# A four-layer graph network kernel: GpSimd's gathers wait for TensorE's signal of two or three batches before

## What is computed

```python
x = _layernorm(x + _L0_gnn_ref(x, edge_index, ...))                 # mean of x[src] over the edges of a node, then a matmul
x = _layernorm(x + _L1_gnn_ref(x, edge_weight, src, dst, ...))      # max over the edges of relu([x[src], x[dst], w] @ W1 + b1) @ W2 + b2
x = _layernorm(x + _L2_gnn_ref(x, edge_index, ...))                 # an edge gate, sigmoid of a small MLP, weighs a normalised sum
x = _layernorm(x + _L3_gnn_ref(x, edge_index, ...))                 # attention, 4 heads of 32, softmax over the edges of a node
```

## Time and profile before

| what | us |
|---|---|
| median of three runs | 5461.31 |
| the profiled execution, time | 5471.71 |
| its span, first to last instruction | 5470.0 |
| TensorE matmuls, busy | 3630.2 |
| VectorE, busy | 3535.5 |
| GpSimd, busy | 3508.5 |
| ScalarE, busy | 1505.4 |
| gathers of the sum pass, first to last start | 5.2 to 1046.7 |
| of the max pass | 1212.5 to 2261.3 |
| of the gate pass | 2469.9 to 3510.5 |
| of the attention pass | 4268.2 to 5309.4 |

### The profile page before, as it was taken

One profiled execution on the slowest core, in us unless ns is written; L12 is line 12 of the kernel. 1 busy time (PEld: TensorE's weight loads), 2 busy tenths in 40 slices (PEclk: granted clock), 3 DMA queues, 4 the chain that ended last, 5 costly groups with the idle time before them and its releaser, 6 DMA issues. The chain is left out here.

```text
span 5470.0 us, 86641 instructions
## 1 busy us (share of the span) xinstructions
PE 3630.2 (66%) x19277; PEld 2699.7 (49%) x19277; DVE 3535.5 (65%) x7296; ACT 1505.4 (28%) x3630; POOL 3508.5 (64%) x3697
## 2 busy tenths in 40 slices
PE   4444333466666666677888888766656688888883
PEld 3333333344443444345666666555542466666662
DVE  6555222227888878615777777799883466666667
ACT  1111111132222222232222222266664122222222
POOL 7777777667777777647777777500006777777763
PEclk7555555568888888765555555598885677777775
DMA  7555555436666667426666666599983676677761
GB/s 234 182 183 180 188 186 179 140 92 198 206 209 208 207 208 207 138 63 164 172 170 170 171 170 169 140 307 306 290 277 116 190 215 213 214 212 218 215 187 50
DMA packets 832058, 1031.70 MB, mean 189 GB/s; under 512 B 233279, under 2 KB 544079, under 8 KB 831954
## 3 DMA queue, kind: packets, MB, share of 16 engines
q1 hardware_dynamic: 482964, 483.11, 29.0%
q0 software_dynamic: 144320, 323.10, 22.6%
q10 hardware_dynamic: 204670, 224.39, 11.6%
HBM read 668.65 MB, written 361.50 MB: 188 GB/s over the span
## 5 line engine op out<-in xcount | busy, mean ns | idle before, releaser
L513 POOL DMA_INDIRECT L_gath<-tab,src x832 | 796.4, 957 | 256.5 <-issue 250.9
L513 POOL DMA_INDIRECT L_gath<-in_x,src x832 | 789.1, 948 | 255.9 <-issue 251.8
L513 POOL DMA_INDIRECT L_gath<-tab_kv,src x832 | 788.9, 948 | 253.6 <-issue 240.2
L513 POOL DMA_INDIRECT L2a_gath<-tab_h,src x832 | 788.3, 947 | 253.8 <-issue 253.8
L616 DVE TENSOR_TENSOR_SCAN L_acc<-L_mask,L_acc,L_pT 128x512 f32<-128x512 bf16 x414 | 527.5, 1274 | 568.5 <-PE L_pT L574 567.5
L1386 POOL DMA_INDIRECT N_got<-run,last x196 | 190.0, 969 | 664.2 <-POOLq L116 605.6
L633 ACT ACTIVATE L_back<-L_pB 128x512 f32<-128x512 f32 x624 | 364.3, 584 | 894.5 <-PE L_pB L604 888.5
L574 PE MATMUL L_pT<-ident,L_gath 128*128 128x128 f32 x832 | 227.4, 427 | 558.9 <-DMA L_gath<-in_x,src 550.0
L604 PE MATMUL L_pB<-ident,L_acc 128*128 128x128 f32 x2496 | 522.8, 349 | 0.8 <-DVE L_acc L616 0.5
L604 PEld LDWEIGHTS L_pB<-ident,L_acc 128*128 128x128 f32 x2496 | 412.1, 185 | 154.0 <-issue 151.9
L574 PEld LDWEIGHTS L_pT<-ident,L_gath 128*128 128x128 f32 x832 | 146.3, 214 | 637.8 <-DMA L_gath<-in_x,src 340.1
(11 more groups left out here) (283 smaller groups left out, 7276.5 us busy)
## 6 DMA issues: line engine op xcount, KB each, us to landing
run<-L_back ACTq DMA_DIRECT2D x416, 256.0 KB, 4.0
L_seed<-seed SPq DMA_DIRECT2D x416, 256.0 KB
run<-L_back ACTq DMA_DIRECT2D x208, 264.0 KB
L_mask<-same SPq DMA_DIRECT2D x416, 128.0 KB, 3.9
seed<-L_zeros SPq DMA_DIRECT2D x208, 256.0 KB, 4.0
sent<-L2a_gath ACTq DMA_DIRECT2D x208, 256.0 KB, 2.9
L_sent<-sent SPq DMA_DIRECT2D x208, 256.0 KB, 4.6
run<-L_back SPq DMA_DIRECT2D x208, 256.0 KB, 4.5
```

Source lines behind the costliest of these rows:

```text
L513: gp.indirect_dma_start(out=gath[k][:, t, :], out_offset=None, in_=table, in_offset=bass.IndirectOffsetOnAxis(ap=g["src"][:, tile:tile + 1 ...
```

## The change

`gatherer` takes a second semaphore and a distance. From batch 32 on (`PACED = 32`) it waits, behind the wait for a free buffer and ahead of the marker, until batch n - 2 is signalled by TensorE (n - 3 in the max pass). In the sum and gate passes the semaphore is the one that frees the buffers too, `s_turn`; in the max pass it is `s_turn` instead of `s_sent`, in the attention pass `s_query` instead of `s_pv`. Nothing else changes: the same instructions on the same engines in the same order, with the same buffers.

```diff
+PACED = 32
...
-def gatherer(gp, g, table, gath, s_gath, s_go, s_free, s_copied=None):
+def gatherer(gp, g, table, gath, s_gath, s_go, s_free, s_pace, ahead, s_copied=None):
...
         room(gp, s_free, n, depth)
+        if n >= PACED:
+            room(gp, s_pace, n, ahead)
         gp.sem_inc(s_go, 1)
...
-            gatherer(gp, g, d["x"], gath, s_gath, s_go, s_turn)
+            gatherer(gp, g, d["x"], gath, s_gath, s_go, s_turn, s_turn, 2)
...
-            gatherer(gp, g, g["tab"], gath, s_gath, s_go, s_sent)
+            gatherer(gp, g, g["tab"], gath, s_gath, s_go, s_sent, s_turn, 3)
...
-            gatherer(gp, g, g["tab_h"], gath, s_gath, s_go, s_turn, s_aside)
+            gatherer(gp, g, g["tab_h"], gath, s_gath, s_go, s_turn, s_turn, 2, s_aside)
...
-            gatherer(gp, g, g["tab_kv"], gath, s_gath, s_go, s_pv)
+            gatherer(gp, g, g["tab_kv"], gath, s_gath, s_go, s_pv, s_query, 2)
```

## The result

The changed kernel takes **5498.51 us** in the median of four runs (5493.1 to 5502.71), beside 5460.97 us for the kernel before: a ratio of 1.0063, 95% interval 1.0051 to 1.0075. It is 37.5 us slower. The prediction said 5466, between 5455 and 5485; the result lies outside.

The account below looks back on a forecast made before the run. The prediction took GpSimd's 1.25 us a gather to bound all four passes. Holds in the sum pass, 17.35 us in full, were cut to 5 and added to the median of 5461.31, giving 5466 us, range 5455 to 5485.

Parts of the forecast that it names:

- What bounds the kernel: All four gather passes: GpSimd writing out gathers sets the end, 1.25 us each, 5.0 us a batch.
- Which passes pay: Max, gate and attention passes: slack over 1.6 us, no cost; sum pass: 49 batches under 0.86, all but one after 108.
- What a wait needs: GpSimd at the new wait: restarts 0.86 us after the signal, so each wait costs max(0, 0.86 - slack).
- Why less than that sum: Sum pass, second half: a held batch's lag gives way, so 49 holds cost 0.1 us each, 5 us instead of 17.35.
- rival (b): Sum pass, second half: lag does not give way; full 17.35 us, 5479, or 24 with 1.0 us start, 5485; chance 0.29.
- the sum itself: Sum pass: 0.86 - slack added over 49 batches, 17.35 us; 3.7 with 0.3 us, 24.2 with 1.0 us.
- What would show it: Sum pass: GpSimd idle put down to TensorE's transposes rises from 1.5 to 5 to 25 us; other passes and gather mean unchanged.
- The rival "faster": DMA queues: fewer gathers in flight relieve them, gaining the max pass's 8 us and a few more, 5452; chance 0.07.

Follow-up runs that it names:

- e2: Changed kernel with the new wait removed from the sum pass, kept in the max, gate and attention passes; ratio 1.0007 to the kernel before.
- e1: Changed kernel with the new wait kept in the sum pass alone; 5510.1 us beside 5472.5, ratio 1.0079 to the kernel before.
- e3: Changed kernel with the sum pass waiting for batch n - 3 instead of n - 2, all passes waiting; ratio 1.001 to the kernel before.
- e4: Changed kernel with the new wait in the sum pass alone and before even batches only; ratio 1.0075 to the kernel before.
- e12: Changed kernel with the new wait in the max and attention passes alone, at 5.47 ms; ratio 1.000 to the kernel before.
- e13: Changed kernel with waits in the max and attention passes alone, at distances five and four; ratio 0.9998 to the kernel before.
- e14: Changed kernel with the wait in the sum pass alone, all zero fills in its first 104 batches; 5522.0 us, ratio 1.008 to the kernel before.
- e5: Changed kernel with waits in the sum pass only, at every tenth batch from 109; ratio 1.0066 to the kernel before, which took 6.8 ms then.
- e7: Kernel before with all zero fills in the sum pass's first 104 batches, no new wait; ratio 0.9995 to the kernel before, at 6.8 ms.

## Why the prediction was wrong

**What bounds the kernel: right.** Every pass is bound by 1.25 us a gather, and a gather that is held moves the end by as much.

**Which passes pay: right.** The sum pass's second half pays (39.5 of 41 us), and the other three passes' waits are free, alone (`e2`) as in the changed kernel. The prediction counted 49 batches with too little slack, and 49 are held; that one of every two is late, and the other at 7.5 us of lag never, was right as well. That these were the odd ones both times is luck, since they are the even ones in the traces of three kernels with the same sum pass.

**What a wait needs: right in kind, 0.06 us too dear.** The prediction took 0.86 us from ScalarE's copy and a scatter; the gathers start 0.797 us after the signal. That would have made the sum smaller: with 0.797 the trace of before gives 14.2 us instead of 17.35.
The Trainium skill, page "DMA: Bandwidth & Descriptors", section "Anatomy of one DMA", gives some 50 ns for the sequencer's dispatch. The runs don't agree that this is what a GpSimd that stands at a wait needs: the 0.797 us are sixteen times as long. With the changed kernel's lags as they are, 0.05 us would give holds of 8 us in all (an estimate from that figure and the trace's lags), and there are 40.

**The failed step: "Why less than that sum".** It reduced 17.35 us to 5, by the reasoning that a held batch's lag gives way, with a slope of 0.80 between neighbouring late lags that puts the steady lag at 9.18 us, 0.1 us a batch. The changed kernel's late lags have a median of 10.0 us, and 9.97 us is the mean lag of its held batches, where the prediction had 9.18 (in `e1` it is 9.65). Their steady cost is 0.82 us a batch, eight times the term. The slope had been taken over 48 pairs of one execution in which nothing was held: it told how a lag follows the one before in a drifting sequence, and was read as what a hold would do. Such a line has a slope of 0.37 to 0.83 in the five other traces whose second half has no hold and has its fills, and gives 9.25 to 9.73 us after a lag of 9.14, so neither the slope nor the 9.18 belongs to the kernel. Nearest to what came is rival (b), which had 0.29: the lag does not give way. Its 17 and 24 us were still too small.

**And the sum itself was mis-sized.** Even the full sum, 17.35 us, is half of what was measured. It rested on the trace of one execution. The same sum over the second half of the sum pass, with 0.797 us, 10.0 us for two batches and the lags as they are, can be made in each trace without holds there: 14.2 us (before), 27.9 (`e2`), 15.0 (`e3`), 26.9 (`e4`), 42.2 (`e12`), 30.9 (`e13`). Late lags have stretches near 9.3 us and stretches near 10.0, with and without holds, and before's trace has mostly the low ones. Since a hold is lag minus 9.18, the 0.7 us between 9.3 and 10.0 make 0.12 us of cost into 0.82. The mean of the six is 26 us; the two traces with holds have 40 us (after) and 25 (`e1`), and the medians of the timed runs are +37.5 and +37.6. Whether the holds themselves add the last 10 us, or the executions happened to be high ones, isn't told apart.

**"What would show it" named the wrong entry.** The holds were to be put down to TensorE's transposes. They are under "issue" (1.5 us are still all that TensorE is named for); that this is so because 0.8 us lie between the signal and the gather is likely, but not shown. Somebody who looks for the name finds nothing; the longest gap of the group (1.7 against 0.3 us) finds them. The other signs came as said: the gathers' mean is 946 to 954 ns against 947 to 957, and the three other passes take 1039 to 1046 us.

**The rival "faster"**, at 0.07, was wrong at 5.47 ms and right on the other occasions, by a way that the earlier trace rows could not show: the gain is not in GpSimd's rate but appears where GpSimd no longer bounds the passes.

## What to carry to other kernels

A wait for a signal of two batches ago is free only if it is met some time before the engine would start: here 0.8 us were needed, and 1.57 us and more cost nothing. Count the slack of every batch, and of both kinds if the batches go in pairs. If the slack is near the price of a restart, a few tenths of a microsecond of lag change the loss severalfold: read the lag in more than one execution, and where there is one trace only, put the full sum in the middle, without a feedback term that nobody has seen at work. Then put the wait where the slack is large: one batch further back cost nothing here, and waits in the two passes with 1.89 us of slack and more were free, and on one occasion worth 2.7%.

## What the runs showed of the hardware

- GpSimd's indirect DMA starts 0.797 us after the last of the transposes for whose signal it stood waiting, alike to about 2 ns over 48 batches of the changed kernel; a queued one follows after 0.30 us.
- In the changed kernel GpSimd's queue spends up to 13.7 us at the marker behind the wait (line 515; 0.04 us at most in the earlier trace rows). The longest begins at 152 us, ahead of batch 32, the first that waits, and no gather there starts late: that costs nothing as long as the gathers already queued last:

```profile
L515 POOLq EVENT_SEMAPHORE  x832: 17/468/13652, 4.2 to 5331.8; - x167
```

- Which of two alternating batches is the late one differs between traces of kernels with the same sum pass, and so does the late lag (medians of 9.37 to 10.06 us in before, `e2`, `e12` and `e13`).
- With the new wait in a pass, some gathers start 0.4 to 1.4 us late in front of the second gather of batches 50, 72, 94 and so on, every 22nd: three in the changed kernel's sum pass, seven in that of `e14` (9.6 us), none in the kernel before or in `e1`. Why is open.
- On some occasions the same kernel takes 6.8 ms instead of 5.47, its gather passes being 1.2 to 1.4 times as long. It is not the chip: under one chip number the kernel before took 5472.5 us beside `e1` to `e4` and 6818.1 beside `e5` to `e7`. There the waits, which keep GpSimd from running ahead, made the max and attention passes 6 to 7% shorter. Why is open.
